# Deformable convolution: one image's odd-row weights read in full width by DMA, the column tents capped on GpSimd, a ring of 18 rows

## What is computed

```python
py = off_y + hs[None, None, :, None] + ky[None, :, None, None]
px = off_x + ws[None, None, None, :] + kx[None, :, None, None]
...
sampled = jax.vmap(sample_one)(x, y0i, x0i, wy, wx)
sampled = sampled * mask[:, None]
out = jnp.einsum('bckhw,ock->bohw', sampled, w.reshape(O, C, KK))
```

## Time and profile before

| | |
|---|---|
| Median of 3 runs | 2212.66 us (2212.55 to 2214.42) |
| Profiled execution, its own time | 2222.19 us |
| Its span | 2219.9 us |
| Sampling stage, first load | 629.67 us of the span |
| Tent stage, issue of its stores (36, 202.72 us) | from 413.70 us |
| TensorE clock granted, mean over the span | 0.867 |

### The profile page before, as it was taken

The page is one execution under the profiler, slowest core; times in us unless marked ns, Lnnn a source line. Parts: engine busy times, 40 slices in busy tenths (PEclk is TensorE's granted clock), DMA queues, the critical chain, the costliest instruction groups (busy, mean ns, idle before and its releaser), DMA issues. The chain is left out here.

```text
span 2219.9 us, 59528 instructions
## 1 busy us (share of the span) xinstructions
PE 1506.6 (68%) x24206; PEld 1036.7 (47%) x24207; DVE 1554.0 (70%) x1718; ACT 1448.5 (65%) x2219; POOL 393.1 (18%) x742
## 2 busy tenths in 40 slices
PE   4745994000018898988898898898898888983430
PEld 4633331000016666666666666666666666662210
DVE  5335001998418888898898888898898898895115
ACT  2211224654118999898899999998899999992002
POOL 2000003664011211112111211211212212111000
PEclk9678997555558999999999999999999999997565
DMA  3087786799964555655555556555465565531008
GB/s 122 12 187 194 207 242 167 226 338 332 309 175 133 160 161 137 172 146 149 160 147 163 148 150 173 141 154 167 133 170 153 142 171 147 151 105 25 3 1 356
DMA packets 191052, 362.29 MB, mean 163 GB/s; under 512 B 54748, under 2 KB 144691, under 8 KB 187205
## 3 DMA queue, kind: packets, MB, share of 16 engines
q1 hardware_dynamic: 165232, 323.10, 50.7%
q0 software_dynamic: 20528, 21.23, 3.5%
q10 hardware_dynamic: 5030, 14.25, 2.1%
HBM read 251.47 MB, written 106.91 MB: 161 GB/s over the span
## 5 line engine op out<-in xcount | busy, mean ns | idle before, releaser
L864 PE MATMUL ps_odd_y<-rows,sel 32*128 32x504 f32 (+1 forms) x896 | 440.8, 492 | 425.2 <-DMA rows<-scratch_parts 282.5
L1005 DVE TENSOR_TENSOR G<-odd_y,ps_odd_v 128x1008 f32<-128x1008 f32 (+2 forms) x464 | 541.7, 1167 | 166.9 <-PE ps_odd_v L881 166.8
L881 PE MATMUL ps_odd_v<-tent_x,stage 32*128 32x171 f32 (+2 forms) x5568 | 580.5, 313 | 0.0
L881 PE MATMUL ps_even_v<-tent_x,stage 32*128 32x171 f32 (+3 forms) x5568 | 534.3, 319 | 11.3 <-DMA stage<-scratch_xt 11.2
L1013 DVE TENSOR_TENSOR G<-even_v,ps_even_y 128x1008 f32<-128x1008 f32 (+2 forms) x464 | 538.4, 1160 | 1.8 <-ACT even_v L959 0.2
L953 ACT COPY odd_y<-ps_odd_y 128x504 f32<-128x504 f32 (+2 forms) x928 | 526.4, 567 | 18.6 <-PE ps_odd_y L864 14.8
L959 ACT COPY even_v<-ps_even_v 128x1008 f32<-128x1008 f32 (+2 forms) x464 | 450.4, 971 | 126.8 <-PE ps_odd_v L881 119.3
L899 PE MATMUL ps_r<-G,conv_w 128*32 128x224 f32 (+1 forms) x8832 | 477.1, 342 | 1.4 <-issue 0.8
L881 PEld LDWEIGHTS ps_odd_v<-tent_x,stage 32*128 32x128 f32 x5568 | 468.4, 186 | 0.4 <-issue 0.4
L864 PEld LDWEIGHTS ps_odd_y<-rows,sel 32*128 32x128 f32 x896 | 164.4, 184 | 598.6 <-ACT odd_y L953 301.1
L881 PEld LDWEIGHTS ps_even_v<-tent_x,stage 32*128 32x128 f32 x5568 | 434.7, 186 | 11.7 <-DMA stage<-scratch_xt 11.5
(11 more groups left out here) (155 smaller groups left out, 1047.9 us busy)
## 6 DMA issues: line engine op xcount, KB each, us to landing
place<-scratch_px SPq DMA_DIRECT2D x768, 147.0 KB, 3.4
rows<-scratch_parts SPq DMA_DIRECT2D x192, 294.0 KB, 4.9
scratch_parts<-parts SPq DMA_DIRECT2D x9, 3136.0 KB, 22.3
scratch_parts<-parts SPq DMA_DIRECT2D x9, 2688.0 KB, 12.2
x<-scratch_xh SPq DMA_DIRECT2D x48, 406.0 KB, 6.2
stage<-scratch_xt SPq DMA_DIRECT2D x192, 96.0 KB, 3.1
scratch_om<-om ACTq DMA_DIRECT2D x64, 196.0 KB, 7.2
scratch_conv<-res POOLq DMA_DIRECT2D x448, 14.0 KB, 1.9
```

The source lines that it names most:

```text
L864: nc.tensor.matmul(ps_odd_y[:, lo:hi], sel[32 * g:32 * g + 32, :], taps(rows, 32 * g, 32, p, lo, hi), start=True, stop=True).then_inc(odd_ ...
L881: m = nc.tensor.matmul(sub(ps_v[g % 2], 0, 128, i * 512 + lo + first, dims), stage[32 * g:32 * g + 32, j * IMAGE + v * C:j * IMAGE + (v + ...
L1005: nc.vector.tensor_tensor(two(G, ROW, v, slot(v)), two(odd_y[p % 3], ROW, v), two(ps_v[1], 512, v), ALU.mult).then_inc(odd_weighted, 1)
```

## The change

1. In the tent stage the row tents of odd view rows of the second image of each pair are no longer stored as 16 kinds (rounded part and remainder) but as the full float32 tent, 8 window rows, written twice side by side into a new DRAM array `full` (`store_full`). It is issued by SyncE once `scaled` tells that the product is there. `parts` keeps its 16 kinds for the other three of four rows.
2. In the sampling stage the second image's odd row weights are loaded from `full` straight into all 128 partitions (`load_wide`, three transfers per batch, each row of 1176 elements read by 8 partitions; `load_last` for the 29th step). `odd_y` is now one tile of three batches: the first holds what ScalarE copies for image 0, the other two are the two buffers for image 1. `spread_odd` and `keep_odd` are done for image 0 alone, `load_rows` loads 48 rows and not 64.
3. `cap` moves from VectorE to GpSimd. `dist_x`, `tent_x` and `even_v` have two buffers and not three.
4. `store` moves from GpSimd to SyncE, at the step in which `result` is made.
5. `G` has 18 rows, counted on through all pairs; in blocks whose first row stands near the ring's end the taps are taken in another order.
6. `ident`, `same_image`, `wm` and `zeros` are freed after the first stages, and the stage for far pixels has zeros of its own.

```diff
-G_SLOTS = 20
+G_SLOTS = 18
...
+            full_stored = [sem(f"full_stored{i}") for i in range(3)]
...
+                def store_full(n):
+                    sp.wait_ge(scaled, n + 1)
+                    for q in range(2):
+                        for block, parity, first, part, npart, row, count in runs(n, q):
+                            for copy in range(2 * parity):
+                                sp.dma_start(dram("full", (block * PAIRS * 2 * WIN + copy) * BATCH + first,
+                                                  [[2 * WIN * BATCH, npart // 2], [2 * BATCH, WIN], [1, count * W]]),
+                                             every_other(tent_y[n % 3], part + 1, npart, q * HALF + row * W,
+                                                         [[DCH, WIN], [1, count * W]])).then_inc(full_stored[n % 3], 16)
...
+                            if parity == 0:
+                                sp.dma_start(there("parts", Y_KINDS, block, parity, first, npart, count * W),
+                                             sub(parts[b], part, npart, q * HALF + row * W, here).bitcast(fp32)
+                                             ).then_inc(stored[b], 16)
+                            else:
+                                sp.dma_start(dram("parts", (block * 2 * B + parity) * Y_KINDS * BATCH + first,
+                                                  [[4 * Y_KINDS * BATCH, npart // 2], [BATCH, Y_KINDS], [1, count * W]]),
+                                             every_other(parts[b], part, npart, q * HALF + row * W, here).bitcast(fp32)
+                                             ).then_inc(stored[b], 16)
...
+                for n in range(KK):
+                    store_full(n)
+                    if n:
+                        store_parts(n - 1)
+                store_parts(KK - 1)
...
+                    wait(act, full_stored[n % 3], full_until(n))
...
-            dist_x = [sb(f"dist_x{b}", ROW) for b in range(3)]
-            tent_x = [sb(f"tent_x{b}", ROW) for b in range(3)]
-            odd_y = [sb(f"odd_y{b}", 2 * ROW) for b in range(3)]
-            even_v = [sb(f"even_v{b}", 2 * ROW) for b in range(3)]
+            dist_x = [sb(f"dist_x{b}", ROW) for b in range(2)]
+            tent_x = [sb(f"tent_x{b}", ROW) for b in range(2)]
+            odd_y, last_odd = sb("odd_y", 3 * BATCH), sb("last_odd", 2 * 3 * W)
+            even_v = [sb(f"even_v{b}", 2 * ROW) for b in range(2)]
...
-            def slot(v):
-                return v % G_SLOTS * 2 * ROW
+            def slot(it, v):
+                return (VIEWS * it + v) % G_SLOTS * 2 * ROW
...
-                        to = bass.AP(tensor=rows[n % 2][:].tensor, offset=ky * PIECE, ap=[[2 * pitch, 64], [1, PIECE]])
+                        to = bass.AP(tensor=rows[n % 2][:].tensor, offset=ky * PIECE, ap=[[2 * pitch, 3 * Y_KINDS], [1, PIECE]])
                         sp.dma_start(to.bitcast(fp32),
                                      dram("parts", (n * B + pair * 2) * 2 * Y_KINDS * BATCH + ky * PIECE,
-                                          [[BATCH, 4 * Y_KINDS], [1, PIECE]])).then_inc(rows_loaded[n % 2], 16)
+                                          [[BATCH, 3 * Y_KINDS], [1, PIECE]])).then_inc(rows_loaded[n % 2], 16)
+
+                def load_wide(pair, n):
+                    for ky in range(3):
+                        sp.dma_start(sub(odd_y, 0, 128, (1 + n % 2) * BATCH + ky * PIECE, [[1, PIECE]]),
+                                     dram("full", (n * PAIRS + pair) * 2 * WIN * BATCH + ky * PIECE,
+                                          [[BATCH, 2 * WIN], [0, C // 2], [1, PIECE]])).then_inc(wide_loaded[n % 2], 16)
+
+                def load_last(pair):
+                    for kx in range(3):
+                        sp.dma_start(sub(last_odd, 0, 128, (3 + kx) * W, [[1, W]]),
+                                     dram("full", pair * 2 * WIN * BATCH + (6 + kx) * GROUP * W,
+                                          [[BATCH, 2 * WIN], [0, C // 2], [1, W]])).then_inc(wide_loaded[2], 16)
...
+                def store(pair, blk):
+                    sp.wait_ge(res_ready, BLOCKS * pair + blk + 1)
+                    b = blk % 2
+                    for j in range(4):
+                        i, h = j // 2, j % 2
+                        sp.dma_start(dram("conv", (pair * 2 + i) * O * HW + (blk * BLOCK + h * UNIT_ROWS) * W,
+                                            [[HW, O], [1, UPX]]), res[b][32 * j:32 * j + O, :]).then_inc(res_stored[b], 16)
...
+                        if p == 1:
+                            wait(sp, odd_weighted, STEPS * it)
+                            load_last(it)
...
+                                sp.wait_ge(odd_weighted, STEPS * it + p)
+                                load_wide(it + (n + 2) // (BATCHES - 1), (n + 2) % (BATCHES - 1))
...
+                        if at := block_of(it, p):
+                            if at[2] == BLOCK // 2 - 1:
+                                store(at[0], at[1])
                 unrolled(PAIRS, body)
+                store(PAIRS - 1, BLOCKS - 1)
...
+                def cap(it, p):
+                    n = STEPS * it + p
+                    pool.wait_ge(distant, n + 1)
+                    wait(pool, sampled, n - 1)
+                    lo, hi = both(p)
+                    nc.gpsimd.tensor_scalar(tent_x[(STEPS * it + p) % 2][:, lo:hi], dist_x[(STEPS * it + p) % 2][:, lo:hi], 1.0, 1.0,
+                                            ALU.min, ALU.subtract).then_inc(tent_ready, 1)
...
+                        if to := ahead(it, p + 2, last):
+                            cap(*to)
+                        if p == GROUP - 2:
+                            pool.wait_ge(distant, STEPS * it + GROUP)
+                            pool.wait_ge(place_loaded[2], it + 1)
+                            pool.tensor_tensor(turn[:, 2:3], turn[:, 4:5], turn[:, 4:5], ALU.add).then_inc(place_read, 1)
+                        if p == GROUP:
+                            pool.wait_ge(even_spread, STEPS * it + GROUP)
+                            pool.wait_ge(rows_loaded[2], it + 1)
+                            pool.tensor_tensor(turn[:, 3:4], turn[:, 4:5], turn[:, 4:5], ALU.add).then_inc(rows_read, 1)
...
-                def spread_odd(it, p, i):
+                def spread_odd(it, p):
                     n = STEPS * it + p
-                    wait(pe, odd_kept, 2 * n + i)
+                    wait(pe, odd_kept, n)
                     lo, hi = columns(2 * p + 1)
-                    g = 2 * i + 1
-                    nc.tensor.matmul(ps_odd_y[:, lo:hi], sel[32 * g:32 * g + 32, :], taps(rows, 32 * g, 32, p, lo, hi),
+                    nc.tensor.matmul(ps_odd_y[:, lo:hi], sel[32:64, :], taps(rows, 32, 32, p, lo, hi),
                                      start=True, stop=True).then_inc(odd_spread, 1)
...
+                    for turn in range(2 * t, KK if t == BLOCK // 2 - 1 else 2 * t + 2):
...
+                                top = BLOCK * blk + UNIT_ROWS * h
+                                k = (turn + 6) % KK if (VIEWS * it + top) % G_SLOTS > G_SLOTS - UNIT_ROWS else turn
+                                v = top + k // 3
+                                whole = min(UNIT_ROWS, G_SLOTS - (VIEWS * it + v) % G_SLOTS)
...
-                            spread_odd(*to, 0)
+                            spread_odd(*to)
                         if at := block_of(it, p):
                             if at[2] == 0:
                                 pe.wait_ge(even_weighted, STEPS * at[0] + BLOCK // 2 * (at[1] + 1) + 1)
                             reduce(*at)
-                        if to:
-                            spread_odd(*to, 1)
                 unrolled(PAIRS, body)
...
-                def keep_odd(it, p, i):
+                def keep_odd(it, p):
                     n = STEPS * it + p
-                    act.wait_ge(odd_spread, 2 * n + i + 1)
-                    if i == 0:
-                        wait(act, odd_weighted, n - 1)
+                    act.wait_ge(odd_spread, n + 1)
+                    wait(act, odd_weighted, n - GROUP + 1)
                     lo, hi = columns(2 * p + 1)
-                    nc.scalar.copy(odd_y[p % 3][:, i * ROW + lo:i * ROW + hi], ps_odd_y[:, lo:hi]).then_inc(odd_kept, 1)
+                    here = sub(odd_y, 0, 128, *odd(0, p, lo, hi)) if p < STEPS - 1 else last_odd[:, 0:3 * W]
+                    nc.scalar.copy(here, sub(ps_odd_y, 0, 128, lo, [[W, (hi - lo) // W], [1, W]])).then_inc(odd_kept, 1)
...
+                    old = STEPS * it + p - G_SLOTS // 2
+                    if old >= 0 and old % STEPS % (BLOCK // 2) == 0 and old % STEPS < STEPS - 1:
+                        dve.wait_ge(reduced, BLOCKS * (old // STEPS) + old % STEPS // (BLOCK // 2) + 1)
...
+                    if p % GROUP == 0:
+                        dve.wait_ge(*arrived(wide_loaded, PER_WIDE, p // GROUP, it))
+                    dve.wait_ge(odd_kept, n + 1)
```

(13 more changed lines are left out.)

128 lines of the change are left out of this document (53 added, 75 removed).

## The result

The changed kernel takes **2231.6 us** (median, 2221.3 to 2241.5) against 2214.7 us for the kernel before on the same chip (2212.6 to 2219.8): a ratio of 1.006, interval 1.0042 to 1.0078. It is slower by 0.6%. The forecast was 2142, its range 2105 to 2192: wrong in sign, and outside the range.

A forecast was written before the change was run, and what follows sets the result against it. The bound was taken to be a loop of waits in the sampling stage, not one engine. -75 + 10 - 5 = -70 from the profiled 2222.19 gave 2152, less 9.5 for the median: 2142 us, range 2105 to 2192.

The forecast's parts named there:

- The DMA queue: Sampling stage: about 19.5 MB a pair takes 67 to 76 of 79.6 us, hidden, with little to spare.
- Rival 4: Sampling stage: the queue becomes the bound; at 225 GB/s 86.7 us a pair, 2256 us in all; chance 0.10.
- Bytes: Queue load per pair: 12.47 MB less 0.9, plus 7.2 wide, 0.35 for the 29th step, 0.4 results: about 19.5 MB.
- The steady step: Sampling stage: a block of four steps takes 11.08 us against 11.74; 4.7 us a pair, 75 us over 16 pairs.
- Loop A: Sampling and the odd product, one bank set `ps_odd_v` between them: 2.66 us from sampling to sampling.
- Loop B: Path through the even product: two successive steps take at least 5.35 us together, 5.73 with the long reduction.
- rival 1: The even-product loop does not bind: steps 2.66 and 2.84, 29 us more saved, 2113 us; chance 0.10.
- The cap on GpSimd: Cap moved off VectorE in sampling: takes 0.6 to 1.2 us; up to 1.8 us costs nothing.
- Rival 3: GpSimd becomes the bound if the cap exceeds some 2.3 us; at 2.4 about 2235 us; chance 0.04.
- `keep_odd`, the odd product, the ring of 18 rows: Sampling stage: one of two copies goes, ScalarE off the path; odd product again 1.20 us; ring zero, up to +3 us.
- Start and tent stage: Sampling starts later behind the wide loads, +10 us; tent stage stores leave earlier, -5 us, between -10 and +8.
- Stores on SyncE at zero: Result stores issued by SyncE behind loads, four issues per block: cost zero.

The follow-up runs named there:

- thin_wide: The changed kernel with the wide loads of pairs 1 to 15 cut from 1176 to 56 elements a row: 2112.9 us, ratio 0.953.
- cap_vector: The changed kernel with the column cap moved back from GpSimd to VectorE, all else kept: 2208.1 us, ratio 0.995.

## Why the prediction was wrong

- **The DMA queue**, "hidden, with little to spare": this step failed. The sum had no term for it, and the bytes of the wide loads cost 119 us (108 with the cap on VectorE). The price of a load was part of it: the rows of `place` (258 GB/s) and `rows` (369) gave 20 to 28 us a pair, and the eightfold form took 29.9, at 242 GB/s; the queue's work was 79 us a pair against 67 to 76. With 128 different rows a wide piece took 203 ns, 19.5 us a pair, which is the fast bound, and then the loads were hidden but for 5 us. The larger part was the word "hidden": at 79 us of work in a pair of 86 the queue was not full on average, and still TensorE had 57 us of issue time that the sum had no place for, the lower clock for 85 us, and VectorE waited 22.5 us for wide loads. That last wait was named as a sign of being wrong. What brings the issue time is open.
- **Rival 4** named the eightfold reading and said 86.7 us a pair; it was 85.9. It had 0.10 because `place` "still reaches 258"; its pieces read one row 32 times and are indeed quicker than the eightfold ones, so the row was of another form. That the two figures are close is in part luck: the rival let the queue fill the pair, and its work stayed at 79 us, below the rival's own limit of 84.3; and with the cap on VectorE a pair is 83.6, quicker than the kernel before. The whole was forecast at 2256 and took 2231.6.
- **Bytes**: 0.35 MB for the 29th step should be 0.09 (3 transfers of 28.0 KB). It changes nothing.
- **The steady step**: right, and better than the sum. Loop A's 2.66 is there (2.64 above). Loop B was said to cost 0.38 behind each long reduction; TensorE took it at 2.6 to 2.8 like the others. A pair was 77.8 in `thin_wide` where 79.6 was forecast, and rival 1's pitch is 78.1. That rival 1 also gave 2113 us and `thin_wide` took 2112.9 is luck to the last figure: the cap costs 13 us there, and the part behind the stage is 12 us shorter.
- **The cap on GpSimd**: 1.85 us on average, 1.89 in the full steps, not 0.6 to 1.2, and just above the slack of 1.8. "Costs nothing" was wrong: in the six pairs of runs that differ in this alone the cap on GpSimd costs 9 to 29 us. Nor was the move needed for loop A: with the cap on VectorE the median step is 2.64 us (`cap_vector`) against 2.69 in the changed kernel. The copy at 593 ns was the wrong neighbour. The Trainium skill, page "GPSIMD Engine Reference", section "Performance versus the Vector engine", has a factor of two, measured on an addition of two inputs; for this operation it was short as well: 4.5. Rival 3's point, 2.3 us, was not reached.
- **`keep_odd`, the odd product, the ring of 18 rows**: right. The odd product is 1.21, and no wait on the ring shows. ScalarE is off the path.
- **Start and tent stage**: the first odd product of the first pair is 6.7 us later (656.32 to 662.99), forecast +5. SyncE issued the first load of the stage 8.8 us earlier (629.67 to 620.90), where 5 was forecast; from there to the first sampling product it took 15.4 us longer, where 10 was. The two misses cancel.
- **Stores on SyncE at zero**: the medians agree, but see above: in the profiles the part behind the last odd product is some 10 us shorter, a term that the sum did not have.

## What to carry to other kernels

When a change trades engine work for loads, price the loads by a row of their own form: how many partitions, how long the pieces, and how many pieces of one transfer read the same place. A broadcast over 8 partitions was slow and one over 4 in two transfers less so; try the split before giving up the idea. Count the issues too: at some 0.59 us each, 155 transfers a pair kept SyncE busy all the time and cost more than the engines did. And where the queue fills, look for idle time put down to issue on TensorE in the middle of a run; half of the longer gaps here also brought a stretch at the lower clock.

## What the runs showed of the hardware that was not expected

- 128 x 4704 bytes from 16 rows, eight readers each: landing 9.7 us, 311 ns a piece. The same from 32 or 128 rows, or from 128 starts inside the same 226 KB: 6.7 to 6.8 us, 203 to 209 ns. Why eight and not four is open; the trace does not tell which of the 16 engines reads which row.
- One row to 32 partitions (`place`): 265 to 274 ns a piece in the kernels compared here. Four readers in 64 partitions: 275. One reader in 16 partitions, 14112 bytes: 1039.
- Loads cut into pieces of 1176 bytes took 65 ns a piece, so four cost less than one of the eightfold pieces; the kernel was 104 us slower while SyncE issued one transfer behind the other, 0.59 us each, for 1194 of 1200 us.
- A gap of 1.62 us in TensorE's work was followed by a granted clock of 0.54 over 3.4 us, one of 1.57 us by none below 1.00; of 27 gaps of 1 us or more, 15 were.
- GpSimd's subtract after a minimum on 128x504 takes 1.89 us in every full step, its copy of as many elements 0.59.
